# A decoder layer with three attention stages: the next pair's scores behind the first steps and the product of the pair in front

## What is computed

```python
x = x + attn(layernorm(x))              # softmax(q k / sqrt(8), causal) v, then out_proj
x = x + xattn(layernorm(x), ctx)        # relu(out @ W1 + b1) @ W2 + b2
x = x + ffn(layernorm(x))
# ffn: h = x + rope_attention(rmsnorm(x, g1)); y = h + moe(rmsnorm(h, g2))
# moe: top 2 of softmax(x @ w_router); silu(x wg) * (x wu) @ wd of those experts
```

## Time and profile before

| | us |
|---|---|
| median of 3 runs | 776.78 |
| lowest, highest | 773.3, 783.43 |
| profiled execution | 777.54 |
| its span, first to last instruction | 775.6 |
| TensorE matmul busy in the span | 631.1 (81%) |
| VectorE busy | 504.5 (65%) |
| ScalarE busy | 380.2 (49%) |
| GpSimd busy | 251.7 (32%) |

### The profile page before, as it was taken

One profiled execution on the slowest core, in us unless ns is written; L12 is line 12 of the kernel. 1 busy time (PEld: TensorE's weight loads), 2 busy tenths in 40 slices (PEclk: granted clock), 3 DMA queues, 4 the chain that ended last, 5 costly groups with the idle time before them and its releaser, 6 DMA issues.

```text
span 775.6 us, 28866 instructions
## 1 busy us (share of the span) xinstructions
PE 631.1 (81%) x11861; PEld 477.7 (62%) x11861; DVE 504.5 (65%) x1196; ACT 380.2 (49%) x765; POOL 251.7 (32%) x361
## 2 busy tenths in 40 slices
PE   3798999999989878897787787868785676999960
PEld 1465666666656546555564554556785566999960
DVE  4386787878776774876676675685464454666645
ACT  4255555566565544472552542532544334777730
POOL 5000110102212324333515425333145553444440
PEclk9599999999999997999899998996798897999995
DMA  5305400100000000000101001000111122222219
GB/s 132 97 17 185 116 24 12 40 26 17 16 27 17 27 23 23 27 17 30 32 9 36 16 9 36 23 10 22 34 45 49 53 66 63 66 65 63 66 45 323
DMA packets 44960, 38.88 MB, mean 50 GB/s; under 512 B 11248, under 2 KB 37424, under 8 KB 44832
## 3 DMA queue, kind: packets, MB, share of 16 engines
q1 hardware_dynamic: 40512, 28.11, 12.4%
q0 software_dynamic: 4320, 8.92, 3.4%
HBM read 18.71 MB, written 12.01 MB: 40 GB/s over the span
## 4 chain that ended last, share of the span: by engine, by line
PE 57%; DVE 19%; issue 10%; ACT 5%; DMA 2%; POOL 2%; another core or an unknown queue 2%; SPq 2%; ACTq 0%; DVEq 0%; POOLq 0%
PE ring L1075 9%; PE ps_s L708 8%; PE ring L1038 7%; PE ps_s L1063 7%; PE ring L1091 6%; DVE rmax L1259 5%; DVE shifted L1263 5%; PE ring L961 4%; PE ring L716 3%; PE ring L952 3%; PE ps_s L1051 3%; PE ring L1018 2%; PE ring L1014 1%; PE ring L1011 1%
## 5 line engine op out<-in xcount | busy, mean ns | idle before, releaser
L1120 ACT ACTIVATE probsT<-ring 128x512 f32<-128x512 f32 x192 | 105.1, 595 | 158.0 <-PE ring L1075 127.2
L1259 DVE TENSOR_REDUCE rmax<-ps_s 128x16 f32<-128x1024 f32 x96 | 117.2, 1221 | 81.4 <-PE ps_s L1063 80.9
L1263 DVE TENSOR_TENSOR shifted<-ps_s,rmax 128x1024 f32<-128x1024 f32 x96 | 117.6, 1225 | 10.6 <-PE ring L1091 0.5
L708 PE MATMUL ps_s<-room 128*128 128x128 f32 x852 | 113.9, 286 | 3.5 <-DVE room L794 1.8
L1075 PE MATMUL ring<-const,shifted 128*128 128x128 f32 x768 | 112.7, 292 | 4.2 <-DVE att L1275 3.0
L1091 PEld LDWEIGHTS ring<-vbd,probsT 128*32 128x32 f32 x6144 | 67.1, 112 | 72.8 <-issue 69.2
L708 PEld LDWEIGHTS ps_s<-room 128*128 128x128 f32 x852 | 107.2, 202 | 4.9 <-issue 4.7
L672 POOL DMA_INDIRECT y_dram<-room x71 | 68.7, 968 | 104.6 <-DVE room L800 97.6
L1091 PE MATMUL ring<-vbd,probsT 128*32 128x18 f32 x6144 | 79.3, 188 | 21.8 <-issue 15.5
L1075 PEld LDWEIGHTS ring<-const,shifted 128*128 128x128 f32 x768 | 88.0, 148 | 9.1 <-DVE shifted L1263 3.0
L791 DVE SCALAR_TENSOR_TENSOR room<-room,ps_s 128x384 f32<-128x384 f32 x71 | 39.3, 553 | 69.5 <-ACT room L762 35.7
(11 more groups left out here) (165 smaller groups left out, 905.3 us busy)
## 6 DMA issues: line engine op xcount, KB each, us to landing
room<-kS SPq DMA_DIRECT2D x96, 64.0 KB
room<-moved_dram SPq DMA_DIRECT2D x71, 65.0 KB
room<-y_dram SPq DMA_DIRECT2D x16, 256.0 KB, 5.8
room<-in_x SPq DMA_DIRECT2D x8, 256.0 KB, 3.3
out<-room SPq DMA_DIRECT2D x8, 256.0 KB, 5.9
cin<-in_ctx SPq DMA_DIRECT2D x8, 192.0 KB, 2.8
w_exp<-in_L_ffn_wg SPq DMA_DIRECT2D x1, 1536.0 KB, 8.4
w_exp<-in_L_ffn_wu SPq DMA_DIRECT2D x1, 1536.0 KB, 11.9
```

What stands on the lines that cost most here:

```text
L708: last = mm(bank[r][:, k * P:(k + 1) * P], w, xbT[r], start=True, stop=True)
L1120: nc.scalar.activation(probsT[p % 2][:, 4 * g:4 * g + 4, :], ring[u.bank][:].rearrange("p (k c) -> p k c", c=P), ACT.Exp, scale=SCALE)\
L1259: V.reduce_max(rmax[p % 2][:].rearrange("p (g k) -> p g k", g=GROUPS), ps_s, AX.X).then_inc(rmax_ready, 1)
L1263: V.tensor_tensor(shifted[p % 2][:].rearrange("p (g k) s -> p g k s", g=GROUPS), ps_s, rmax[p % 2][:].rearrange("p (g k) -> p g k", g=GROU ...
```

## The change

In every slot the scores and the shift of the pair that follows stand behind the first steps and the product of the pair in front, where they stood at the slot's start.

```diff
@@ -209,14 +209,14 @@
     for n in range(N_JOBS):
         for p in range(SUB):
             following = (n, p + 1) if p < SUB - 1 else (n + 1, 0)
-            if following[0] < N_JOBS:
-                scores(*following)
-                shift(*following)
             steps(steps_at(n, p, 0))
             if p > 0:
                 attend(n, p - 1)
             elif n > 0:
                 attend(n - 1, SUB - 1)
+            if following[0] < N_JOBS:
+                scores(*following)
+                shift(*following)
             exps(n, p)
             steps(steps_at(n, p, 1))
     attend(N_JOBS - 1, SUB - 1)
```

## The result

The changed kernel takes 774.45 us (median of 20 runs, 765.84 to 777.49), the kernel before beside it 778.82 us (20 runs, 773.3 to 784.11). The ratio is 0.9943, 95% interval 0.9922 to 0.9965. A second measurement of the changed kernel gave 772.28 us and 0.9896 (0.9853 to 0.9939). So the change is worth 4 us and perhaps up to 8, not the 12 of the forecast. The profiled execution took 770.58 us.

The account below looks back on a forecast made before the run. TensorE was taken to set the pace, so its idle time in the loop was what could change. Gains of 17.5, 10.5 and 3.3 us less 21.5, plus small `att` waits of 2.1, made 12: about 765 us, range 746 to 788.

Parts of the forecast that it names:

- Gain 1: Normalising ahead of the maximum on VectorE: all 17.5 us of TensorE's listed waits for `att` go, bounds 0 to 17.5.
- Gain 2: Scores later on TensorE: of 13.8 us of waits for `shifted` some 3.3 stay, gain 10.5 us, bounds 5 to 13.8.
- The loss: Scores no longer cover the eviction of `xT` before k or q in 15 jobs: 21.5 us net, bounds 12 to 30.
- the rotary jobs: R1, R5, R7: RMS scaling on ScalarE delays the `xT` eviction, 2.0 to 3.6 us each, 3.3 taken, 9.9 us in all.
- Gain 3: Evictions of q and k of a rotary job now stand before the shift on VectorE: 3.3 us of waits go.
- The part behind 541 us is as before, only earlier.: The program after the slot loop keeps its length and only starts earlier: no change in size.
- The 15.5 us with the releaser "issue" inside the value product have no named cause, and I leave them where they are.: TensorE's "issue" waits within the product with the values in the loop: 15.5 us taken as unchanged.
- The marks: Signs to check in the profile after: TensorE's waits by kind, second-part clock 0.90 to 0.93, last A ending near 530 us.
- The clock did not come back: Rival 1: fewer waits bring the second part's granted clock from 0.91 to 0.98, saving 16 us more, 749 us; chance 0.20.
- The exponentials are covered: Rival 2: A waits for T's exponentials, 13 us, about 778 or up to 786 us; chance 0.26 together with rival 4.
- The third rival: Uncovered `xT` evictions in C4 to C7, R1, R5, R7 also lower the clock: 777 to 794 us; chance 0.12 with worse variants.
- VectorE was late anyway: Rival 4: in the second part gain 1 returns as waits elsewhere, about 775 us; chance 0.26 together with rival 2.

Follow-up runs that it names:

- cut kernels: Old and new order without the 71 expert blocks and the last sum: 600.82 and 597.85 us; also without the 64 indirect transfers: 546.38 and 537.32 us.
- after_again: The changed kernel, unaltered, measured and profiled a second time: 772.28 us.

## Why the prediction was right and wrong

**Direction right, size wrong.** 765 us was forecast, 12 less than before; 774.45 was measured, 4.4 less, above the 757 to 773 of the forecast's own chance. The exchange of waits in the loop came as described. Gain 1 came: 18.6 us of waits for `att` gone, forecast 19.6. Gain 2 came: 10.2 us, forecast 10.5, and what stays is where it was put, 0.66 us in the first slot and 1.64 at 504.32, the place of the earlier trace rows where the choosing of experts comes together with statistics. The loss came in exactly the 15 places that were named, with the causes that were named; it was sized 21.5 and measured 16.8, because the rotary jobs cost 2.1 us each and not 3.3, and the four cross jobs 6.25 in all and not 7.4. The chain of the rotary jobs starts on VectorE; that VectorE got earlier too is argued, not measured. I had bounded them by 2.0 and 3.6, and the value taken, 3.3, had no row behind it.

**Gain 3: eaten.** The waits for the rotary evictions went as forecast, but a new one of 3.2 us came at 280.29, in job C4, where T waits for the eviction of `wo` (L1338). Both kernels in turn, first the one before:

```profile
276.98 0.77 DVE L511 TENSOR_TENSOR carried<-carried,sel 128x8 f32<-128x8 f32 x4
...
277.67 0.69 DVE L1338 TENSOR_TENSOR room<-ring,room 128x512 f32<-128x512 f32 x1
...
278.75 1.09 PE L1075 MATMUL ring<-const,shifted 128*128 128x128 f32 x8
```

```profile
277.68 1.87 DVE L511 TENSOR_TENSOR carried<-carried,sel 128x8 f32<-128x8 f32 x4
...
279.47 0.68 DVE L1338 TENSOR_TENSOR room<-ring,room 128x512 f32<-128x512 f32 x1
...
280.29 1.94 PE L1075 MATMUL ring<-const,shifted 128*128 128x128 f32 x8 [3.19 <-DVE room L1338]
```

T needs the bank that this eviction frees. Before, v had waited 2.48 us for `att` ahead of it, and VectorE used that time for the choosing of experts. Now v waits 0.17 us, TensorE is at T early, and the wait has moved to the next thing that VectorE has to deliver; its four small additions (L511) took 1.1 us longer as well. The prediction has no term for this wait, nor for one of 1.1 us for the eviction of `hres` at 500.01.

**The steps that failed.** Two terms were put at nothing without a reason.

The first: "The part behind 541 us is as before, only earlier." In the two pairs of profiled executions it is 3.4 and 7.3 us longer. The mean of the two pairs is 4.8 us shorter, close to the 4.4 of the medians, so they can be used to split the miss: the loop brought 10.8 of the 12 us that were forecast, the part behind it gave 5.4 back, and the loop started 0.6 later. So most of what is missing from 12 us is missing behind the loop. Its cause is open. The cut kernels show no such lengthening, and there it is the last job that loses the gain.

The second: "The 15.5 us with the releaser "issue" inside the value product have no named cause, and I leave them where they are." They were the largest row, and I took them for a constant. They are not one: together with their like ahead of other instructions they grew from 21.6 to 27.3 us, and all but some 4 us of them stand beside the row moves on GpSimd and are gone where these are left out. In the loop's sum this 5.7 us was made good by the smaller loss at `xT` (4.7) and by less busy time (3.8). In the kernel before, part of the moves' time fell on other engines. The old kernel's timeline at its moves of job C6, and behind the eight moves that it issues from 520.01 to 529.92:

```profile
368.22 0.96 POOL L1452 DMA_INDIRECT moved_dram<-moved,pos_i  x1 [0.31 <-issue]
369.57 1.28 ACT L1120 ACTIVATE probsT<-ring 128x512 f32<-128x512 f32 x2 [5.23 <-issue]
...
531.44 0.26 DVE L1273 RECIPROCAL rden<-ring 128x16 f32<-128x16 f32 x1 [8.76 <-remote]
531.56 1.08 ACT L1120 ACTIVATE probsT<-ring 128x512 f32<-128x512 f32 x2 [12.72 <-remote]
```

("remote" is a releaser that the profile doesn't follow.) At the first place it was ScalarE that was held up, for 5.23 us, and TensorE's wait for it is the 2.22 us for `probsT` in the earlier trace rows. At the second, ScalarE stood still for 12.72 us and VectorE for 8.76. So the idle time of TensorE under "issue" is only a part of what stands still at the moves. In the changed kernel the waits for `probsT` are smaller (5.2 to 1.6 us) and "issue" has grown. That the one took the other's place is argued from these rows; that the growth comes from the moves is shown in the cut kernels, by one profile of each: without them "issue" grows by 1.2 us (3.7 to 4.9), with them by 6.5 (19.5 to 26.0).

What the runs show together is that with the moves the order gains 3 to 8 us, by medians and ratios, and without them 9 in the cut kernel. That the moves, of which 24 are issued behind the loop, also lengthen that part of the whole kernel was not tested.

**The marks.** `att` near 0 and `shifted` under 4 us were met (0.9 and, without the last T, 3.6), `xT` at 20 to 25 just missed (19.9 in 15 places), `probsT` under 8 was met, and the clock at 0.90 just so (0.89 in `after_again`). "The end of the last product near 530 instead of 542" rested on a misreading: the product at 541.49 in the kernel before is the last but one, the last ends at 548.97. It now ends at 538.66.

**The rivals.** The clock did not come back (0.90): the waits that went were replaced by others. That it can come back in this loop is shown by the kernels without the moves, 0.97. The exponentials are covered, waits for them fell. The third rival, that the clock falls, came in small: in the second part the new order has the lower clock in every pair, 0.90 for 0.91, 0.89 for 0.90, 0.88 for 0.90 with the cut and 0.95 for 0.97 without the moves. By the prediction's own reckoning a hundredth is 0.01 x 2 x 281 x (1 - 1/1.7) = 2.3 us, an estimate; that the uncovered evictions are its cause was not tested. VectorE was late anyway in two places only, where 3.2 and 1.1 us of the 18.6 came back as waits for its evictions.

## What to carry to other kernels

When two engines pass work back and forth, move a pair of calls on both queues or on neither: each half alone cost 80 and 142 us here, the whole gained 4. After such a move look for the short step whose result the next instruction needs (`xT` and its k) and leave something between the two; that, with the scaling moved, was worth 12 to 14 us more (760.27 against 772.28 and 774.45 us). Read the part behind the changed loop as well: here it gave back half of what the loop gained (5.4 of 10.8 us in the mean of two profiled pairs). And a row of waits without a named cause is a term of the sum: look for what happens on the other engines at the same times before taking it as fixed.

## What the hardware showed that I had not expected

- 64 indirect transfers issued by GpSimd, of some 0.96 us each, cost a kernel of 600 us 54 us, though nothing in it reads what they write. While they are issued TensorE's small matmuls come in bursts of 2 to 6 with 0.45 to 1.20 us between, with the releaser "issue". The other engines stand still longer: in the loop of the kernel before, while moves are issued (61 us, to 1 us behind each group), ScalarE is busy 20% of the time, VectorE 40% and TensorE 65%, against 44, 67 and 80% from 260 to 545 us as a whole.
- They also make the time scatter: the two cut kernels range over 8.1 and 9.8 us with them and over 1.6 and 3.7 us without.
- The clock was higher without them: 0.97 in the second part of the cut kernel, 0.90 with them, for the same order of instructions.
